# A decoder layer with routed experts on one core: row buffers twice, the first stage one step deeper, two expert loads late

## The chip, the cores and the metric

One core of a Trainium2 chip runs the whole layer in one launch. The metric is the device time of a run in microseconds (us). Three runs of the kernel before took 887.20, 883.02 and 879.79 us; the median is 883.02 us.

## The reference, cut to what matters

The input is x, 16 sequences of 256 tokens of width 256 (float32), and a context of the same shape. Three parts follow each other; each adds its input and normalizes it.

```python
# 1 attention of every sequence on itself
q, k, v = x@Wq.T + bq, x@Wk.T + bk, x@Wv.T + bv
qk = einsum('bsd,btd->bst', q, k)
theta = 0.5 + 0.2*sigmoid(qk) + 0.15*tanh(qk) + 0.1*relu(qk)
x1 = layernorm(x + (softmax(theta) @ v) @ Wo.T + bo)
# 2 cross attention to the context, 16 heads of 16, in chunks of 64 tokens
x2 = layernorm(x1 + out_proj(chunk_attention(x1, ctx)))
# 3 experts: 32 of them, 4 for each token, and a shared one
topk_idx, topk_w = route(x2)                  # sigmoid, best 2 of 4 groups, best 4 experts
h = silu(x2 @ gate_w[e].T) * (x2 @ up_w[e].T) # for the chosen experts e
out = layernorm(x2 + sum_e topk_w * h @ down_w[e].T + shared(x2))
```

## The kernel before, in words

All is float32. There are two stages, and a short last one.

**The first stage** goes over the 16 sequences in a software pipeline: `for t in range(nseq + 5)`, written out once for each engine (TensorE "PE" line 706, ScalarE "ACT" line 955, VectorE "DVE" line 1296, GpSimd "POOL" line 1413, the DMA queue of SyncE "SP" line 1490). In step t the engines work on sequence t (attention on itself: z, vo, scores1, prT, av1, x1T, and the context's k and v, and q), on sequence t-1 (cross attention: scores2, pTa, pTb, den, av2, spread, out2), on t-3 (router, shared expert, choice of experts, rank) and on t-4 (shared_out, and the scatter of the rows). Each engine works its list in the order in which it is written, and nothing overtakes; semaphores join the engines (`wait_ge`, and `after`, which waits only where the value is positive). The eight PSUM banks are shared out by hand, so many waits of PE stand for a bank that has to be read first.

In step t PE works in this order before: scores2(t-1), x2T(t-3), z, vo, scores1(t), shared_out(t-4), router, gate(t-3), pTa(t-1), k(t), prT(t), pTb(t-1), av1(t), up(t-3), av2, den(t-1), v(t), rank(t-3), x1T(t), spread(t-1), q(t), out2(t-1).

**Rows.** The normalized x2 of a sequence is copied four times, once for each chosen expert, into `row`, one buffer of [128, 4, 2, 258] (256 values, the weight, the number of the row in the result). POOL does this in `pool_row` (line 1377, copies at line 1382). DVE then writes weight and indices in `vec_key` (line 1178), and POOL scatters the rows to a DRAM tensor `routed`, sorted by expert, with eight indirect DMAs for each sequence (lines 1398 and 1405, "scattera" and "scatterb"). `pool_row` of the next sequence waits until all eight have landed. In POOL's list the order of a step is xc(t), rs2(t-3), scattera(t-4), xc2(t-1), scatterb(t-4), rs1(t), row(t-3). `act_norm2` (line 907) makes x2; what it needs from POOL is rs2.

**Queues.** SP issues the loads of the next sequence (xT, x, context), the store of the shared expert's part (`store_acc`), and `load_rest` (line 1463): in step 1 a write of 4128 KB of zeros to `routed` (line 1468), and in steps 1 to 16 the weights of two experts each (768 KB, line 1472). SP works in order too.

**The second stage** (`pe_tables` and the loops over 159 blocks of 128 rows) starts when the last scatter has landed: SP waits for it (lines 1503 and 1504) and then reads the first block (line 1511). PE also waits for all weights (`ld_we`). The last stage sums four results for each token and normalizes.

## Time and profile before

| | us |
|---|---|
| median of three runs (lowest, highest) | 883.02 (879.79, 887.20) |
| the profiled execution | 873.37 |
| its span | 871.2 |
| PE busy | 801.1 (92%) |
| DVE busy | 546.1 (63%) |
| ACT busy | 461.5 (53%) |
| POOL busy | 408.3 (47%) |

The span is the time from the first to the last thing that the profiler saw; the profiled execution took 2.2 us more than its span. "Busy" is the time in which an engine had an instruction in work. Matmuls are pipelined and overlap, so a busy PE says that it did not wait, not that it ran at its peak. The profile also gives the granted clock of TensorE as a share of full speed.

### The profile page before, as it was taken

The numbers are of one execution on the slowest core, as the hardware profiler recorded it, in microseconds if no ns is written. First come the engines' busy times: TensorE is split into PE (matmuls) and PEld (weight loads), VectorE is DVE, ScalarE is ACT, GpSimd is POOL, SyncE is SP. The second block draws the span as 40 slices with busy tenths as digits, with TensorE's granted clock in tenths as the row PEclk, the third lists the DMA queues.
The fourth block names the chain that finished last, engine by engine and source line by source line (L and its number), as shares of the span: only waits on it lengthen the run. The fifth ranks groups of instructions, "written<-read, shape, count | busy, mean of one in ns | idle before, by whom it ended". The sixth has DMA issues, their size and how long they took to land.

```text
span 871.2 us, 23658 instructions
## 1 busy us (share of the span) xinstructions
PE 801.1 (92%) x7881; PEld 658.8 (76%) x7881; DVE 546.1 (63%) x2115; ACT 461.5 (53%) x1150; POOL 408.3 (47%) x501
## 2 busy tenths in 40 slices
PE   7778999999999999999999555899999999999885
PEld 6567788888888888888887444688888888887332
DVE  2244577887788787887788852355555555554366
ACT  1455566655665666655665111466666666665133
POOL 0200235464455546464545662455656555556123
PEclk9999999999999999999999875999999999999999
DMA  6472223243324322342331124855555555552996
GB/s 222 125 174 79 80 69 103 100 136 93 121 76 142 106 103 82 133 124 94 104 127 58 67 86 134 301 163 166 165 162 159 169 165 158 161 170 91 327 401 242
DMA packets 69654, 125.06 MB, mean 144 GB/s; under 512 B 9665, under 2 KB 43329, under 8 KB 69282
## 3 DMA queue, kind: packets, MB, share of 16 engines
q1 hardware_dynamic: 51394, 81.60, 30.3%
q0 software_dynamic: 13776, 37.77, 12.1%
q10 hardware_dynamic: 4368, 4.20, 1.4%
q8 instruction: 67, 1.10, 0.5%
q14 instruction: 49, 0.40, 0.2%
HBM read 73.16 MB, written 50.36 MB: 142 GB/s over the span
## 4 chain that ended last, share of the span: by engine, by line
PE 78%; DMA 6%; POOL 5%; issue 4%; SPq 4%; ACT 2%; DVE 1%; ACTq 0%; POOLq 0%; DVEq 0%
PE banks L584 15%; PE banks L274 11%; PE banks L597 7%; PE banks L393 4%; SPq L623 4%; PE banks L381 3%; PE banks L354 3%; PE banks L314 3%; PE banks L335 3%; PE banks L371 3%; PE banks L326 3%; PE banks L487 3%; PE banks L518 3%; PE banks L541 3%; PE banks L529 3%
## 5 line engine op out<-in xcount | busy, mean ns | idle before, releaser
L1431 POOL DMA_INDIRECT y<-yb_tile,idcol_tile x159 | 153.0, 962 | 123.6 <-ACT yb_tile L948 121.3
L584 PE MATMUL banks<-w_expert_tile,xbT_tile 128*128 x636 | 166.4, 385 | 3.9 <-ACT xbT_tile L786 3.9
L584 PEld LDWEIGHTS banks<-w_expert_tile,xbT_tile 128*128 128x128 f32 x636 | 109.9, 193 | 13.5 <-issue 4.9
L1259 DVE COPY hbT_tile<-banks 128x128 f32<-128x128 f32 x159 | 46.4, 292 | 117.2 <-PE banks L274 117.2
L1398 POOL DMA_INDIRECT routed<-row_tile,idx_tile x64 | 63.3, 989 | 85.0 <-PE banks L410 66.5
L948 ACT ACTIVATE yb_tile<-banks,rowsb_tile 128x256 f32<-128x256 f32 x159 | 75.4, 474 | 48.8 <-PE banks L597 41.5
L597 PE MATMUL banks<-w_expert_tile,hbT_tile 128*128 x318 | 95.7, 383 | 0.0
L1366 POOL TENSOR_TENSOR rs_tile<-ve_tile,half_neg_tile 128x2 f32<-128x2 f32 x16 | 11.5, 717 | 140.6 <-DVE ve_tile L1046 140.6
L1405 POOL DMA_INDIRECT routed<-row_tile,idx_tile x64 | 65.7, 1027 | 17.7 <-issue 17.7
L942 ACT ACTIVATE gb_tile<-banks 128x128 f32<-128x128 f32 x159 | 44.2, 278 | 55.5 <-PE banks L584 55.5
L786 ACT ACTIVATE xbT_tile<-banks 128x256 f32<-128x256 f32 x159 | 59.9, 377 | 25.5 <-PE banks L274 25.2
L274 PE MATMUL banks<-const_tile,rowsb_tile 128*128 128x128 f32 x318 | 62.0, 278 | 6.9 <-DMA rowsb_tile<-routed 6.9
L274 PEld LDWEIGHTS banks<-const_tile,rowsb_tile 128*128 128x128 f32 x318 | 45.4, 144 | 23.9 <-DMA rowsb_tile<-routed 7.7
L597 PEld LDWEIGHTS banks<-w_expert_tile,hbT_tile 128*128 128x128 f32 x318 | 48.3, 192 | 12.6 <-issue 0.8
L649 PE MATMUL banks<-w_expert_tile,const_tile 128*128 128x512 f32 (+1 forms) x102 | 45.7, 596 | 8.1 <-DMA w_expert_tile<-y 8.1
L1242 DVE SCALAR_TENSOR_TENSOR hb_tile<-gb_tile,banks 128x128 f32<-128x128 f32 x159 | 44.6, 280 | 9.7 <-ACT gb_tile L942 9.6
L1246 DVE TENSOR_TENSOR hb_tile<-hb_tile,banks 128x128 f32<-128x128 f32 x159 | 45.6, 287 | 5.6
L649 PEld LDWEIGHTS banks<-w_expert_tile,const_tile 128*128 128x128 f32 x102 | 19.1, 196 | 35.2 <-DMA w_expert_tile<-y 17.8
L274 PE MATMUL banks<-const_tile,hb_tile 128*128 128x128 f32 x159 | 43.5, 274 | 0.0
L693 ACT ACTIVATE w_expert_tile<-w_expert_tile,fnmr_tile,frs_tile 128x256 f32<-128x256 f32 x32 | 17.6, 593 | 47.2 <-DVE fnmr_tile L673 47.2
L1382 POOL COPY row_tile<-x_tile 128x512 f32<-128x512 f32 x64 | 37.5, 625 | 6.9 <-DMA routed<-row_tile,idx_tile 6.9
L1360 POOL TENSOR_TENSOR xc_tile<-x_sb_tile,c_out_tile 128x256 f32<-128x256 f32 x32 | 23.0, 741 | 31.2 <-DVE c_out_tile L1311 27.4
(205 smaller groups left out, 1847.0 us busy)
## 6 DMA issues: line engine op xcount, KB each, us to landing
rowsb_tile<-routed SPq DMA_DIRECT2D x159, 129.0 KB, 2.2
w_expert_tile<-y SPq DMA_DIRECT2D x15, 1024.0 KB, 16.6
w_expert_tile<-w_expert SPq DMA_DIRECT2D x16, 768.0 KB, 6.3
cT_tile<-ctxT SPq DMA_DIRECT2D x16, 384.0 KB, 3.4
routed<-zrow_tile SPq DMA_DIRECT2D x1, 4128.0 KB, 22.7
xT_tile<-xT SPq DMA_DIRECT2D x16, 256.0 KB, 3.2
x_sb_tile<-x SPq DMA_DIRECT2D x16, 256.0 KB, 3.5
base<-acc_sb_tile SPq DMA_DIRECT2D x16, 256.0 KB, 3.8
```

Source lines behind the costliest of these rows:

```text
L274: return e.transpose(o, i, ident)
L584: m = e.matmul(bank[2 + u % 2][:, 0:2 * EI], xbT[u % 2][:, k * P:(k + 1) * P], w_flat[:, bass.ds(w + k * D, D)], start=k == 0, stop=k == D ...
L597: e.matmul(bank[6 + u % 2][:, 0:D], hbT[u % 2][:, :], w_flat[:, bass.ds(w + 2 * D, D)], start=True, stop=True).then_inc(SEM["p_down"], 1)
L649: m = e.matmul(sum_rows(g), ident, part(g, k), start=k == 0 and g >= 8, stop=k == TOPK - 2)
L786: e.activation(o, i, ACT.Copy).then_inc(SEM[done], 1)
L948: e.activation(yb[n % YS][:, :], bank[6 + u % 2][:, 0:D], ACT.Copy, scale=rowsb[n % ROWS][:, D:D + 1])\
L1242: e.scalar_tensor_tensor(hb1[u % 2][:, :], gb[u % 2][:, :], 1.0, bank[2 + u % 2][:, 0:EI], ALU.add, ALU.mult).then_inc(SEM["v_hb1"], 1)
L1246: e.tensor_tensor(hb[u % 2][:, :], hb1[u % 2][:, :], bank[2 + u % 2][:, EI:2 * EI], ALU.mult)\
L1259: e.tensor_copy(hbT[u % 2][:, :], bank[4 + u % 2][:, 0:EI]).then_inc(SEM["v_hbT"], 1)
L1398: e.indirect_dma_start(routed, bass.IndirectOffsetOnAxis(ap=idx[:, 0, k:k + 1], axis=0), row[:, k, 0, :], None).then_inc(SEM["st_rowa"], 16)
L1405: e.indirect_dma_start(routed, bass.IndirectOffsetOnAxis(ap=idx[:, 1, k:k + 1], axis=0), row[:, k, 1, :], None).then_inc(SEM["st_rowb"], 16)
L1431: e.indirect_dma_start(y, bass.IndirectOffsetOnAxis(ap=idcol[n % ROWS][:, :], axis=0), yb[n % YS][:, :], None).then_inc(SEM[f"st_y{n % YS} ...
```

## The change

`row` and `idx` become two buffers, taken in turn by even and odd sequences, and each has its own semaphores for the landed scatters. The four POOL copies become one ScalarE instruction, `act_row`, that reads x2 with a broadcast and writes all four copies (128 x 2048 elements). The pipeline is one step deeper, `range(nseq + 6)`: in step t the engines work on t (z, vo, scores1, k, v, prT, av1), t-1 (x1T, q), t-2 (all of cross attention), t-4 (router, gate, up, choice, rank) and t-5 (shared_out). kM, vM, mxa, rs1, nmr1, rs2, nmr2, r_sb, r_half, r_neg and den become two buffers each, rden becomes one. The PSUM banks are shared out anew, with new waits in nearly every function of PE. To make room, t12, prT, x1T and the second kM lie where the weights of the last four experts go, so these weights (the last two loads of 768 KB) are issued in steps 17 and 18 instead of 15 and 16, after waits for the last scores2, q, av1 and pr.

The orders of a step are written anew. PE: x2T(t-4), scores2(t-2), z, vo, scores1(t), router(t-4), k(t), gate(t-4), x1T(t-1), pTa, pTb(t-2), shared_out(t-5), v(t), den, av2, spread(t-2), up, rank(t-4), q(t-1), prT(t), out2(t-2), av1(t). ACT: x2T(t-4), z(t), norm1(t-1), vo(t), sha(t-2), tanh(t), sc(t-4), shb, pTa, pTb(t-2), x1T(t-1), pr(t), row(t-4), gates(t-4), num(t-2), norm2(t-3), q(t-1), prT, v, k(t). DVE: mxa(t-2), r(t), sha, mxb, shb(t-2), th(t), route(t-4), acc(t-5), rden(t-2), choice, hs1(t-4), o(t-2), key, hs2(t-4), x2(t-2), x1(t). POOL and SP stand in the diff. The second and the last stage are not changed.

The diff, cut to its core (bank numbers and waits of most PE functions are left out; two of them stand as examples):

```diff
@@ -143,51 +144,59 @@
+        SHARE = E // nseq * 3 * D
+        LATE = 3072 // SHARE
+
+        def late(at, n):
+
+            return w_flat[:, (nseq - LATE) * SHARE + at:(nseq - LATE) * SHARE + at + n]
...
+        t12 = late(0, 1024).rearrange("p (j t s) -> p j t s", j=2, t=T)
...
+        prT = late(1024, 512).rearrange("p (t u q) -> p t u q", t=T, u=T)
...
+        nmr1 = [sa(f"nmr1{u}", [P, T]) for u in range(2)]
...
+        x1T = late(2560, 512).rearrange("p (k s) -> p k s", k=DK)
...
-        kM = sa("kM", [P, DK, S // CH, 2, CH])
-        vM = sa("vM", [P, T, NP, VW])
-        mxa = sa("mxa", [P, 4, 4])
+        kM = [sa("kM0", [P, DK, S // CH, 2, CH]),
+              late(1536, 1024).rearrange("p (k n h c) -> p k n h c", k=DK, n=S // CH, h=2)]
+        vM = [sa(f"vM{u}", [P, T, NP, VW]) for u in range(2)]
+        mxa = [sa(f"mxa{u}", [P, 4, 4]) for u in range(2)]
...
-        row = sa("row", [P, TOPK, T, RW])
+        row = [sa(f"row{u}", [P, TOPK, T, RW]) for u in range(2)]
...
-        idx = sa("idx", [P, T, TOPK], I32)
+        idx = [sa(f"idx{u}", [P, T, TOPK], I32) for u in range(2)]
...
         def pe_z(e, i):
             e.wait_ge(SEM["ld_xT"], 16 * (i + 1))
-            after(e, SEM["a_pTb"], i - 1)
-            after(e, SEM["v_key"], i - 3)
             after(e, SEM["v_mx"], i)
+            after(e, SEM["v_ve2"], i - 2)
             for db in range(DK):
                 for k in range(DK):
-                    m = e.matmul(bank[1][:, db * S:(db + 1) * S], g_qk[:, k, db * P:(db + 1) * P], xT[:, k, :],
+                    m = e.matmul(bank[7][:, db * S:(db + 1) * S], g_qk[:, k, db * P:(db + 1) * P], xT[:, k, :],
                                  start=k == 0, stop=k == DK - 1)
             m.then_inc(SEM["p_z"], 1)
...
         def pe_vo(e, i):
             e.wait_ge(SEM["ld_xT"], 16 * (i + 1))
-            after(e, SEM["a_prT"], i)
-            after(e, SEM["a_q"], i)
-            after(e, SEM["a_x2T"], i - 2)
-            after(e, SEM["v_o"], i - 1)
+            after(e, SEM["a_k"], i)
+            after(e, SEM["a_q"], i - 1)
+            after(e, SEM["a_vo"], i)
+            after(e, SEM["a_x2T"], i - 3)
             for t in range(T):
                 for k in range(DK):
-                    m = e.matmul(bank[(0, 7)[t]][:, 0:D + 1], xT[:, k, t * P:(t + 1) * P],
+                    m = e.matmul(bank[(1, 6)[t]][:, 0:D + 1], xT[:, k, t * P:(t + 1) * P],
                                  g_vo[:, k, :], start=k == 0, stop=k == DK - 1)
             m.then_inc(SEM["p_vo"], 1)
...
@@ -398,9 +409,13 @@
             e.wait_ge(SEM["a_q"], i + 1)
             e.wait_ge(SEM["a_k"], i + 1)
             after(e, SEM["a_pTa"], i)
-            after(e, SEM["a_v"], min(i + 1, nseq))
-            after(e, SEM["a_x1T"], min(i + 1, nseq))
+            after(e, SEM["a_pTb"], i)
+            after(e, SEM["a_prT"], min(i + 2, nseq))
+            after(e, SEM["a_v"], min(i + 2, nseq))
             after(e, SEM["v_hs"], i - 2)
+            after(e, SEM["v_key"], i - 2)
+            after(e, SEM["v_o"], i)
+            after(e, SEM["v_rden"], i)
             for t in range(T):
                 for hf in range(DK):
                     for a in range(2):
...
         def pe_spread(e, i):
             e.wait_ge(SEM["v_rden"], i + 1)
-            after(e, SEM["v_rden"], min(i + 1, nseq))
+            after(e, SEM["a_pTb"], min(i + 1, nseq))
...
+        def act_row(e, i):
+            e.wait_ge(SEM["a_x2"], i + 1)
+            after(e, SEM[f"st_rowa{i % 2}"], 16 * TOPK * (i // 2))
+            after(e, SEM[f"st_rowb{i % 2}"], 16 * TOPK * (i // 2))
+            e.activation(row[i % 2][:, :, :, 0:D],
+                         x2[i % 2][:, :, :].rearrange("p (k t) d -> p k t d", k=1).to_broadcast([P, TOPK, T, D]), ACT.Copy)\
+                .then_inc(SEM["a_row"], 1)
 
         def act_norm2(e, i):
...
         def act_norm2(e, i):
             e.wait_ge(SEM["g_rs2"], i + 1)
-            after(e, SEM["g_row"], i - 1)
+            after(e, SEM["a_row"], i - 1)
...
@@ -1193,12 +1215,13 @@
             ch(e.tensor_tensor(mine[:, :, :, :], mine[:, :, :, :],
                                wraw[:, :, :].rearrange("p t (k x) -> p t k x", k=1).to_broadcast([P, T, TOPK, E]),
                                ALU.mult))
-            after(e, SEM["st_rowa"], 16 * TOPK * i)
-            after(e, SEM["st_rowb"], 16 * TOPK * i)
-            e.wait_ge(SEM["g_row"], i + 1)
-            e.tensor_scalar(idx[:, :, :], slot[:, :, 0:TOPK], -1.0, None, ALU.add).then_inc(SEM["v_idx1"], 1)
-            e.tensor_scalar(row[:, :, :, D + 1].bitcast(I32), row[:, :, :, D + 1].bitcast(I32), float(T), None, ALU.add)
-            e.tensor_reduce(row[:, :, :, D].rearrange("p k t -> p t k"), mine[:, :, :, :], AX.X, ALU.add)\
+            after(e, SEM[f"st_rowa{i % 2}"], 16 * TOPK * (i // 2))
+            after(e, SEM[f"st_rowb{i % 2}"], 16 * TOPK * (i // 2))
+            e.wait_ge(SEM["a_row"], i + 1)
+            e.tensor_scalar(idx[i % 2][:, :, :], slot[:, :, 0:TOPK], -1.0, None, ALU.add).then_inc(SEM["v_idx1"], 1)
+            e.tensor_scalar(row[i % 2][:, :, :, D + 1].bitcast(I32), row[i % 2][:, :, :, D + 1].bitcast(I32), float(2 * T), None,
+                            ALU.add)
+            e.tensor_reduce(row[i % 2][:, :, :, D].rearrange("p k t -> p t k"), mine[:, :, :, :], AX.X, ALU.add)\
...
-
-        def pool_row(e, i):
-            e.wait_ge(SEM["a_x2"], i + 1)
-            after(e, SEM["st_rowa"], 16 * TOPK * i)
-            after(e, SEM["st_rowb"], 16 * TOPK * i)
-            for k in range(TOPK):
-                m = e.tensor_copy(row[:, k, :, 0:D], x2[i % 2][:, :, :])
-            m.then_inc(SEM["g_row"], 1)
...
         def _(e):
-            e.iota(dest_id[:, :, :], [[N, TOPK], [1, T]], base=-T, channel_multiplier=TILES).then_inc(SEM["g_iota"], 1)
+            e.iota(dest_id[:, :, :], [[N, TOPK], [1, T]], base=-2 * T, channel_multiplier=TILES).then_inc(SEM["g_iota"], 1)
             e.wait_ge(SEM["v_setup"], 3)
             e.wait_ge(SEM["v_const"], 1)
-            for t in range(nseq + 5):
-                if live(t):
-                    pool_xc(e, t)
-                if live(t - 3):
-                    pool_rs2(e, t - 3)
+            for t in range(nseq + 6):
+                if live(t - 2):
+                    pool_rs1(e, t - 2)
+                if live(t - 1):
+                    pool_xc(e, t - 1)
+                if live(t - 6):
+                    pool_scatterb(e, t - 6)
                 if live(t - 4):
-                    pool_scattera(e, t - 4)
-                if live(t - 1):
-                    pool_xc2(e, t - 1)
-                if live(t - 4):
-                    pool_scatterb(e, t - 4)
-                if live(t):
-                    pool_rs1(e, t)
-                if live(t - 3):
-                    pool_row(e, t - 3)
+                    pool_rs2(e, t - 4)
+                if live(t - 6):
+                    pool_scattera(e, t - 6)
+                if live(t - 2):
+                    pool_xc2(e, t - 2)
             for n in range(BLOCKS):
...
@@ -1468,9 +1484,13 @@
                     e.dma_start(routed.rearrange("(e r) w -> r e w", e=E)[0:P, :, :],
                                 zrow[:, :].rearrange("p (e w) -> p e w", e=1).to_broadcast([P, E, RW]))\
                         .then_inc(SEM["st_zrow"], 16)
-                share = E // nseq * 3 * D
-                e.dma_start(w_flat[:, bass.ds(i * share, share)],
-                            d["w_expert"].rearrange("p e n -> p (e n)")[:, bass.ds(i * share, share)])\
+                if i == nseq - LATE:
+                    e.wait_ge(SEM["p_s2"], nseq)
+                    e.wait_ge(SEM["p_q"], nseq)
+                    e.wait_ge(SEM["p_av1"], nseq)
+                    e.wait_ge(SEM["a_pr"], nseq)
+                e.dma_start(w_flat[:, bass.ds(i * SHARE, SHARE)],
+                            d["w_expert"].rearrange("p e n -> p (e n)")[:, bass.ds(i * SHARE, SHARE)])\
...
@@ -1496,12 +1516,16 @@
                     load_c(e, t)
                 if live(t - 5):
                     store_acc(e, t - 5)
-                if live(t - 1):
+                if 0 < t <= nseq - LATE:
                     load_rest(e, t - 1)
+                if nseq < t <= nseq + LATE:
+                    load_rest(e, t - 1 - LATE)
             e.wait_ge(SEM["v_adr"], 1)
             e.wait_ge(SEM["st_zrow"], 16)
-            e.wait_ge(SEM["st_rowa"], 16 * TOPK * nseq)
-            e.wait_ge(SEM["st_rowb"], 16 * TOPK * nseq)
+            for u in range(2):
+                e.wait_ge(SEM[f"st_rowa{u}"], 16 * TOPK * nseq // 2)
+            for u in range(2):
+                e.wait_ge(SEM[f"st_rowb{u}"], 16 * TOPK * nseq // 2)
             for n in range(BLOCKS):
                 if n % UNROLL == 0:
...
```

## Rows read from the trace of the kernel before

**Rows 1.** The page: PE's busy share in tenths, in 40 equal slices of the span.
```profile
PE   7778999999999999999999555899999999999885
```

**Rows 2.** Stretches of the span: start:end, length, busy us (instructions) by engine, clock, DMA.
```profile
0.00:98.40 98.40, 78.00 (x829) 64.39 (x829) 35.16 (x99) 43.04 (x103) 12.30 (x25) 0.95 0.49 145
98.37:465.50 367.13, 366.91 (x5089) 320.26 (x5088) 294.29 (x1064) 226.61 (x521) 185.43 (x250) 1.00 0.32 103
353.20:381.50 28.30, 28.23 (x397) 24.75 (x392) 22.41 (x83) 17.44 (x40) 15.02 (x20) 1.00 0.35 107
465.50:532.00 66.50, 39.06 (x421) 30.84 (x420) 45.86 (x192) 10.92 (x19) 42.65 (x50) 0.81 0.23 80
```

**Rows 3.** Timeline of POOL, 478 to 520 us: start, length, instruction, idle before it.
```profile
481.87 2.50 POOL L1382 COPY row_tile<-x_tile 128x512 f32<-128x512 f32 x4 [3.08 <-DMA routed<-row_tile,idx_tile]
...
497.75 2.50 POOL L1382 COPY row_tile<-x_tile 128x512 f32<-128x512 f32 x4 [1.74 <-DMA routed<-row_tile,idx_tile]
...
519.51 0.98 POOL L1398 DMA_INDIRECT routed<-row_tile,idx_tile  x1 [0.98 <-DVE row_tile L1201]
```

**Rows 4.** Chain of waits at the change of stages: start, length, what.
```profile
528.50 2.48 DMA routed<-row_tile,idx_tile
...
532.00 2.06 DMA rowsb_tile<-routed
```

**Rows 5.** Timeline of PE in the first steps.
```profile
32.12 2.02 PE L381 MATMUL banks<-w_cross_tile,cT_tile 128*128 128x128 f32 x16
...
36.91 0.66 PE L274 MATMUL banks<-const_tile,x_tile 128*128 128x128 f32 x4 [2.77 <-ACT x_tile L903]
...
51.99 1.89 PE L274 MATMUL banks<-const_tile,sha_tile 128*128 128x128 f32 x8 [2.61 <-ACT sha_tile L875]
53.67 2.81 PE L371 MATMUL banks<-cT_tile,w_cross_tile 128*128 128x256 f32 x8
```

**Rows 6.** Timeline of PE in a full step: z and vo, each eight matmuls.
```profile
353.69 1.89 PE L314 MATMUL banks<-xT_tile,g_qk_tile 128*128 128x256 f32 x8
...
355.42 1.90 PE L326 MATMUL banks<-g_vo_tile,xT_tile 128*128 128x257 f32 x8
```

**Rows 7.** Timeline of SP's DMA issues in steps 0 and 1.
```profile
34.64 0.40 SPq L1468 DMA_DIRECT2D routed<-zrow_tile  x1
35.09 12.18 SPq L1472 DMA_DIRECT2D w_expert_tile<-w_expert  x1
49.41 0.33 SPq L1443 DMA_DIRECT2D xT_tile<-xT  x1
```

**Rows 8.** DMA issues of 35 to 50 us, with KB and us from issue to landing.
```profile
routed<-zrow_tile SPq DMA_DIRECT2D x1, 4128.0 KB, 22.7
w_expert_tile<-w_expert SPq DMA_DIRECT2D x1, 768.0 KB, 24.0
xT_tile<-xT SPq DMA_DIRECT2D x1, 256.0 KB, 10.4
```

**Rows 9.** Page, DMA issues of the whole run.
```profile
w_expert_tile<-w_expert SPq DMA_DIRECT2D x16, 768.0 KB, 6.3
xT_tile<-xT SPq DMA_DIRECT2D x16, 256.0 KB, 3.2
```

**Rows 10.** Instructions of ACT, by shape: busy, mean ns, idle before.
```profile
L875 ACT ACTIVATE sha_tile<-sha_tile 128x1024 f32<-128x1024 f32 x16 | 17.1, 1071 | 3.2 <-DVE sha_tile L1073 3.2
L786 ACT ACTIVATE num_tile<-banks 128x512 f32<-128x512 f32 x16 | 9.6, 603 | 18.3 <-PE banks L464 18.3
```

**Rows 11.** Timeline of DVE, 478 to 510 us, and rden of a full step (first row).
```profile
345.57 0.54 DVE L1096 RECIPROCAL rden_tile<-banks 128x64 f32<-128x64 f32 x1
...
485.17 0.68 DVE L1108 TENSOR_TENSOR xc_tile<-banks,xc_tile 128x512 f32<-128x512 f32 x1
...
490.18 0.20 DVE L1117 TENSOR_SCALAR sc_tile<-sc_tile 128x64 f32<-128x64 f32 x1 [0.32 <-ACT sc_tile L921]
...
500.71 0.41 DVE L1201 TENSOR_REDUCE row_tile<-mine_tile 128x8 f32<-128x256 f32 x1
```

428 lines of the change are left out of this document (215 added, 213 removed).

## The prediction

> **What bounds the kernel now.** I read the page first. PE is at 9 tenths from slice 4 on, with one hole at about 470 to 560 us, at the end of the first stage [rows 1]. The table of stretches says more [rows 2]. From 98.4 to 465.5 us PE stands still for only 0.2 of 367.1 us: these are 13 full steps, and one takes 28.3 us, in which PE is busy for 28.2, DVE for 22.4, ACT for 17.4 and POOL for 15.0. The fill, 0 to 98.4 us, holds 78.0 us of PE work. The drain, 465.5 to 532.0 us, holds 39.1 us of work in 66.5, at a clock of 0.81.
>
> The timeline of POOL shows what bounds the drain [rows 3]. The copies of one sequence start at 481.9, those of the next at 497.8: 15.9 us a sequence. Before them POOL has waited 3.1 and 1.7 us for the scatters to land, because there is one row buffer. rs2 stands behind the copies, and ACT's next x2, with the router behind it, waits for rs2. So copies, eight scatters and the landing run one after the other. Eight scatters take 10.2 us: the first of the last sequence starts at 519.5, the eighth at 528.5 [rows 3, 4], which is 1.28 us each. They land at 531.0, and SP reads the first block at 532.0 [rows 4]. From first scatter to that read is 12.5 us.
>
> **The sum in three parts.** "Before" is the profiled execution.
>
> Full steps. PE's work is the same, matmul for matmul, and POOL's 2.5 us of copies [rows 3] leave an engine that isn't the bound: nothing is gained there as long as PE covers all else. Added on ACT is one instruction of 2048 elements. 512 elements take 0.60 us and 1024 take 1.07 [rows 10], so it takes about 1.07 + 2 x 0.47 = 2.0 us, 19.4 of 28.3 in all. It stands between pr and gates. I laid ACT's new list against PE's new one with eight matmuls at 1.73 to 1.8 us [rows 6]: with x2T at 0, pTb ends at 13.6 and av2 at 19.3. ACT then does pTb, x1T, pr until 16.2, row until 18.2, gates until 18.8, and num can't start before 19.3. So row costs nothing; if it took 4.0 us it would still end before q's matmuls, the next that need the bank of num (22.5). Behind it, ACT ends v at 27.7 where scores2 of the next step wants it at 28.9. Not seen before are the new waits. Their bounds are 0 and, if a list is out of tune, the stalls in the second rival; I take 0, since every wait I placed ends 0.1 us or more before its use. The tightest is rden: den ends at 18.3, the reciprocal takes 0.54 [rows 11], the semaphores some 0.3, and spread wants it at 19.25.
>
> Fill. Before, step 0 runs through x1T and q of the same sequence, and PE waits for x1 (2.8 us) [rows 5]. That wait goes, since x1T and q belong to the next step now. Step 0 ends with v done earlier and av1 last, near 33.6, where v ended before at 34.1 [rows 5]. Step 1 has z, vo, scores1, k, q, av1 (six times 1.8), v (2.0) and two sets of four transposes (0.5 each) [rows 5, 6]: 13.8 us, and about 1.0 for the copy of prT on ACT ahead of av1. It ends at 48.4, scores2 at 49.6. What is late next is xT of sequence 2. SP issues the 4128 KB of zeros at 34.6 and the expert weights behind them, and is itself held in that issue for 12.2 us [rows 7]; they landed at 57.3 and 59.1, and xT, issued at 49.4, at 59.8 [rows 7, 8]. Now the zeros go out when v of sequence 0 is done, at about 30.4 instead of 34.1, so all this moves up by 3.5 us only: xT lands at 56.3, and PE waits 6.7 us. Step 2 has 13.8 us as step 1, pTa and pTb 1.8, den, av2, spread 3.0 and out2 1.8: 20.4. After the wait of 2.6 us before, eight transposes that take 1.04 elsewhere took 1.9 and the eight matmuls of k 2.8 instead of 1.9 [rows 5]: the clock was down, which costs about 2. Step 3 adds scores2 (1.2). So 56.3 + 20.4 + 2 + 21.6 = 100.3 us. Now the first step with x2T starts, as before at 98.4, but 12 instead of 13 steps are left to the end of step 15: 367.1 - 28.3 = 338.8. The drain begins at 439.1 instead of 465.5.
>
> The row of xT can be read in two ways: it queued behind the zeros, or it shared the bandwidth. The Trainium skill (DMA: Bandwidth & Descriptors, "Queues, rings and completion order") says that each DMA engine consumes the descriptors of a ring in ring order. By it the load has to wait for what is ahead, as in the sum. If it shared instead, a load issued at 43.8 (zeros at 30.9, weights at 31.3 and SP held for 12.2, then xT) would take its 10.4 us and land at 54.2, and the wait would be 2.1 us shorter.
>
> Drain. It is longer, since two cross attentions are left instead of one. Before, the step with scores2(15) took from 465.5 to the start of x2's last work at 485.2 [rows 11] and 2 us of statistics: 21.7. Two such steps, bound by DVE and PE in turn, overlap to 41.5 (21.9 and 19.6). Then come two steps with routing alone. DVE's chain of one, from route to the end of key, was 490.2 to 501.1, with acc ahead of it: 11 us [rows 11]. So key of the last sequence is ready at 63.5. POOL needs 10.2 us of scatters and 1 of rs2 for each, and has sequences 11 to 15 to do. Key ends 2.7 us (hs2 and x2) before the end of the two long steps, and 0.7 before that of the next, so I place 12 at 19.2 to 30.3, 13 at 38.8 to 49.9 (each with an rs2 between), 14 at 51.8 to 62.0; 15 starts at 63.5 and the read follows 12.5 later, at 76.0. Here the second buffer works: row(15) needs the scatter of 13, not of 14. The ends of this are 72 (DVE's key at its undisturbed length) and 82 (landings as slow as 4 us, slow clock in two steps). I add 1.5 us of slow clock, since the drain before ran at 0.81 [rows 2]: 77.5.
>
> The two late loads: they are issued behind store_acc of 12 and 13, about 31 and 46 us into the drain. One lands in 6.3 us [rows 9], so by 53 of 77.5. Their four waits are for PE and ACT work that is done by 22 us, and the stores behind them on SP aren't held. If that cover were gone, 6 us each. They may slow a landing by a few us; only row(15), with 5 us to spare, sees it.
>
> Sum: 439.1 + 77.5 = 516.6 us to the first read, against 532.0: 15.4 less. The second and last stage, 339.2 us, stay. The span would be 855.8, the profiled time 858.0. The profiled execution, 873.4, is 1.1% under the median of 883.0 and under all three runs; less 15.4 the median is 867.6. I forecast 868.
>
> **Rivals.**
>
> *The fill does not wait* (10%). If xT came before the zeros, 6.7 us and the slow clock's 2 go too: 859. Against it stands the landing 0.7 us after the weights.
>
> *PE loses its cover in the full steps* (13%, slower). Place: DVE's new list, mxa, r, sha, mxb, shb, th, route, acc, rden. Each waits for the one before, and rden stands behind route, about 3.6 us, and acc, which waits for shared_out at 15.4. If sc from ACT came 1 us later, rden would too, and spread, q, out2, av1, then x1 and the next step's sha would shift. From 15.4 / 12 = 1.3 us a step on the gain is gone. At 2.3 us, a whole th late (its four instructions), 27.6 are lost and 15.4 gained: 895. For it: PE had no gap before, so every microsecond shows. Against it: DVE has 5.9 us free in each step, ACT 8.9 with row.
>
> *The drain hands it back* (17%, about the same). If the scatters still went at 15.9 us a sequence, since the landing or x2 is tied as before, 13 to 15 would start at 35, 51 and 67 and the read come at 79.5 or, with late loads in the way of each landing (2 us each), 86: 8.5 more than forecast, 876. That would be the case in which the second buffer doesn't do what it is for.
>
> *The forecast's own case* (60%): 860 to 875, which leaves 0 to 0.6 us of stall in a full step.
>
> **How the numbers follow.** The forecast is 868. The range takes in the fill without wait (859) less the median's own play (the three runs lie within 7.4 us) and, above, the drain that hands it back (876) and mild stalls of up to 0.8 us a step (9.6: 878) with the same play: 857 to 883. It leaves out the strong stall. One per cent is 8.8 us, about what a measurement can tell here. Faster by that or more (under 874.2): forecast's case mostly (0.53 of 0.60), the fill (0.10), part of the rest (0.09): 0.72. Within: 0.17. Slower: 0.11.
>
> **What would show it.** The drain begins at 437 to 442 us, after 12 full steps of 28.3; if these are longer, the second rival is right, and the row of spread, pTa or q names what is late. PE waits about 6.7 us once, before z of step 2, for xT. `act_row` takes 2.0 us. In the drain, scatters of 14 and 15 follow each other almost without a gap, and ACT's row(15) waits for the scatter of 13. The first block is read at 513 to 521. I am wrong if PE shows gaps between 100 and 440, if the zeros end later than 54, or if the drain takes over 82.

## The result, and the profile after

The changed kernel is slower. Four runs took 924.09 us in the median (918.04 to 932.03) and four of the kernel before 881.40 (878.60 to 887.20). The ratio is 1.0453 of before, 95% interval 1.0367 to 1.0538; it is one of means and leaves out the slow run, 932.03. The forecast was 868 us.

The page has PE's busy share in tenths. Before, the nines ran on from slice 4 to the end of the first stage [rows 1]; now they break off again and again.

```profile
PE   7969889999987999989898885899999999999895
```

The table of stretches, cut where fill, full steps and drain end (start:end, length, busy us with instructions by engine, clock, DMA share, GB/s):

```profile
0.00:109.30 109.30, 88.07 (x888) 73.65 (x888) 41.79 (x117) 50.88 (x128) 13.66 (x27) 0.94 0.49 147
109.30:490.30 381.00, 348.81 (x4699) 306.49 (x4697) 272.52 (x985) 223.22 (x492) 142.40 (x184) 0.98 0.26 87
490.30:576.78 86.48, 64.04 (x749) 51.64 (x748) 60.40 (x258) 28.08 (x39) 43.91 (x50) 0.82 0.28 96
```

Twelve full steps take 381.0 us, 31.75 each, where 28.3 was forecast. PE is busy for 348.8 of them, so it stands still for 32.2 us; before, for 0.2 in 367 [rows 2]. PE is also busy for ten us more than 12 x 28.23; the mean granted clock of 0.98 over 381 us, against 1.00 before, accounts for about eight of them. The account, by the sums of the prediction, in us:

| | forecast | measured | more |
|---|---|---|---|
| x2T of the first sequence begins (end of the fill) | 100.3 | 108.9 | 8.6 |
| 12 full steps | 338.8 | 380.9 | 42.1 |
| drain, to the first block read | 77.5 | 87.0 | 9.5 |
| first block read | 516.6 | 576.8 | 60.2 |

The second and last stage took 345.8 us in this execution and 339.2 in that of before. The difference is not of the change: of the experiments, 1 to 4 show 346 to 348 and 5 to 17, which were run later, 338 to 340, and new and old kernels are among the later ones. So of the 51.4 us between the two profiled executions, 44.8 lie in the first stage. What else differs between the two sets of runs matters below, for den.

What PE waits for in the full steps (engine, what it was about to do, what it waited for: us in total, times, longest):

```profile
PE banks L458 <- issue: 12.3, 14, 1.2
PE banks L489 <- issue: 11.5, 6, 3.6
PE banks L520 <- ACT vo_tile L838: 4.2, 12, 0.5
PE banks L562 <- issue: 2.0, 1, 2.0
```

"issue" is a wait that no semaphore of the program explains. L458 is den, L489 spread, L562 rank. The timeline of PE in one step shows where they lie:

```profile
281.25 0.25 PE L458 MATMUL banks<-sha_tile,const_tile 128*32 128x64 f32 x2
...
282.94 0.22 PE L458 MATMUL banks<-shb_tile,const_tile 128*32 128x64 f32 x1 [1.15 <-issue]
...
284.53 0.94 PE L489 MATMUL banks<-rden_tile,const_tile 128*32 128x64 f32 x50
289.09 0.42 PE L489 MATMUL banks<-rden_tile,const_tile 128*32 128x64 f32 x14 [3.61 <-issue]
289.45 3.00 PE L542 MATMUL banks<-x2T_tile,w_shared_in_tile 128*128 128x256 f32 x8
```

PE stops in the middle of den and in the middle of spread, after 50 of 64 passes of matmuls that need nothing new. Behind the long gap up takes 3.00 us instead of 1.9: the granted clock was 1.00 until 290, 0.64 from 290 to 291 and 0.50 from 291 to 293 us, which is the lower level of 1.2 GHz for most of up, after 3.6 us of standing still. Den is not held by DVE. Its reciprocal (L1118) is what waits: 31.3 us in 12 steps, for den.

```profile
L1118 DVE RECIPROCAL rden_tile<-banks 128x64 f32<-128x64 f32 x12 | 6.7, 558 | 31.3 <-PE banks L458 31.3
```

What SP issues in the same step, and then, in the table of stretches of 1 us each (columns as above), how full the DMA engines are:

```profile
281.16 0.33 SPq L1476 DMA_DIRECT2D base<-acc_sb_tile  x1
281.52 0.48 SPq L1492 DMA_DIRECT2D w_expert_tile<-w_expert  x1
282.54 0.33 SPq L1459 DMA_DIRECT2D xT_tile<-xT  x1
282.92 0.49 SPq L1464 DMA_DIRECT2D x_sb_tile<-x  x1
283.50 0.55 SPq L1470 DMA_DIRECT2D cT_tile<-ctxT  x1
```

```profile
284.00:285.00 1.00, 1.00 (x88) 1.00 (x80) 0.90 (x5) 0.20 (x1) 0.00 (x0) 1.00 1.06 412
285.00:286.00 1.00, 0.48 (x33) 0.32 (x21) 0.90 (x6) 1.00 (x3) 0.00 (x0) 1.00 0.95 380
286.00:287.00 1.00, 0.00 (x0) 0.00 (x0) 0.56 (x1) 0.37 (x1) 0.49 (x1) 1.00 1.06 384
287.00:288.00 1.00, 0.00 (x0) 0.00 (x0) 0.00 (x0) 0.00 (x0) 0.91 (x2) 1.00 1.05 387
288.00:289.00 1.00, 0.00 (x0) 0.00 (x0) 0.00 (x0) 0.00 (x0) 0.00 (x0) 1.00 0.35 122
```

All loads of a step (256 + 768 + 256 + 256 + 384 KB = 1.9 MB) now go out in one bundle. In the kernel before, the context, the stored part and the weights went out at 346.7 to 347.5 and xT and x at 359.1 to 359.5. The cause is SP's order: `store_acc(t - 5)` kept its place in SP's list while acc moved in DVE's from t-4 to t-5. So SP stands in that store until the middle of the step, and the loads of the next step behind it. While the engines are full PE doesn't move, and it goes on when they become free.

### The profile page after: what moved, and what is told of

Read it like the earlier page. It is cut to its first block, busy times and chain, and to the rows that moved or that the text cites. A ratio compares the mean times of both kernels' runs of the same rounds, so it can differ in the third digit from the quotient of the medians.

```text
span 922.6 us, 23626 instructions
## 1 busy us (share of the span) xinstructions
PE 824.2 (89%) x7881; PEld 675.8 (73%) x7881; DVE 544.7 (59%) x2117; ACT 480.9 (52%) x1166; POOL 367.3 (40%) x437
## 3 DMA queue, kind: packets, MB, share of 16 engines
q1 hardware_dynamic: 51394, 81.60, 28.3%
## 4 chain that ended last, share of the span: by engine, by line
PE 70%; issue 9%; DMA 6%; SPq 5%; DVE 5%; ACT 3%; POOL 2%; another core or an unknown queue 0%; ACTq 0%; DVEq 0%; POOLq 0%
PE banks L596 13%; PE banks L283 10%; PE banks L609 8%; SPq L635 3%; PE banks L404 3%; PE banks L322 3%; PE banks L542 3%; PE banks L392 3%; PE banks L499 3%; PE banks L553 3%; PE banks L381 3%; PE banks L363 2%; PE banks L458 2%; PE banks L531 2%; DMA w_expert_tile<-y 2%
## 5 line engine op out<-in xcount | busy, mean ns | idle before, releaser
L1423 POOL DMA_INDIRECT routed<-row_tile,idx_tile x64 | 62.9, 983 | 38.1 <-issue 17.5
L1416 POOL DMA_INDIRECT routed<-row_tile,idx_tile x64 | 62.5, 977 | 22.6 <-issue 22.6
L881 ACT ACTIVATE qT_tile<-banks,b_cross_tile 128x256 f32<-128x256 f32 x32 | 13.4, 470 | 77.3 <-PE banks L404 77.3
L1409 POOL TENSOR_TENSOR xc_tile<-x_tile,c_out_tile 128x256 f32<-128x256 f32 x32 | 22.5, 722 | 75.7 <-issue 52.9
```

Source lines behind the costliest of these rows:

```text
L1416: e.indirect_dma_start(routed, bass.IndirectOffsetOnAxis(ap=idx[i % 2][:, 0, k:k + 1], axis=0), row[i % 2][:, k, 0, :], None).then_inc(SEM ...
L1423: e.indirect_dma_start(routed, bass.IndirectOffsetOnAxis(ap=idx[i % 2][:, 1, k:k + 1], axis=0), row[i % 2][:, k, 1, :], None).then_inc(SEM ...
```

## What could stop PE without a semaphore

Three things hold for these gaps. Nearly all fall among short matmuls or just behind them, where PE runs through 192 matmuls and 192 weight loads in some 3 us: den, av2 and spread stand directly behind each other now, where before v, rank and x1T stood between den and spread. In spread their place drifts and comes back every fifth step, three or four passes further on:

```profile
130.62 0.52 PE L489 MATMUL banks<-rden_tile,const_tile 128*32 128x64 f32 x18 [2.55 <-issue]
161.61 0.86 PE L489 MATMUL banks<-rden_tile,const_tile 128*32 128x64 f32 x42 [0.77 <-issue]
...
321.33 0.76 PE L489 MATMUL banks<-rden_tile,const_tile 128*32 128x64 f32 x39 [0.80 <-issue]
...
448.61 0.64 PE L489 MATMUL banks<-rden_tile,const_tile 128*32 128x64 f32 x11 [3.58 <-issue]
481.20 0.75 PE L489 MATMUL banks<-rden_tile,const_tile 128*32 128x64 f32 x36 [0.22 <-issue]
```

With the one at 289.09, of 14 passes, these are pairs five steps apart: 18 and 14 and 11 passes left, 42 and 39 and 36. A semaphore would stop PE at the same instruction in each step; this place counts instructions. And the kernel before has the same kind of gap, in its fill, where no up stands ahead of av2 and den, with the DMA engines idle from 61 to 63 us:

```profile
63.00 0.25 PE L447 MATMUL banks<-sha_tile,const_tile 128*32 128x64 f32 x2 [1.88 <-issue]
```

The page lists a DMA queue for instructions, 67 packets with 1.10 MB, 16.4 KB each. So the theory (A) is: PE's instructions come by DMA in blocks; a run of short instructions uses up a block before the next is there, and full DMA engines make that later. The rivals: B, only the run counts; C, only the DMA counts; D, since the gap in den stands at nearly one place, after 20 to 23 of 64 passes (after 28 in the first step that has it), that one has another cause, POOL's scatters, of which the eighth runs beside it. In the first of the 12 full steps no scatter runs yet, and den has no gap.

A is more than a guess, since the trace holds every packet of that queue. The long gap above lasts from 285.48 to 289.09 us. The queue's last packet before it started at 272.3, the next at 286.83, and PE went on 1.27 us after that one had landed. Here is what the queue of instructions moved in 286.8:287.9 (packets, MB, share of the engines):

```profile
q8 instruction: 1, 0.02, 5.6%
```

It is PE's queue: 38 of its packets fall in the 12 full steps, one for each 247 of PE's matmuls and weight loads, and all six gaps in spread, the one in rank and the one in q end 1.3 to 1.5 us after such a packet has landed. The gaps in den do not follow it: that of 281.79 to 282.94 has no packet of this queue within 8 us before it or 3 us behind it. So A is shown for spread, rank and q, and not for den.

The Trainium skill (Runtime: NRT & Kernel Launch, "Instruction fetch mechanics") describes blocks of 16 KiB that a sequencer fetches through its own DMA queue, and calls the cost "mostly hidden". The size of the packets agrees; the 11.5 us of gaps in spread do not.

## Experiments

Ratios are to runs of the kernel before on the same chip, with 95% intervals. Medians of before lay at 880 us beside experiments 1 to 4 and at 870 beside the later ones, so only ratios are compared. The changed kernel and 1 to 4 are the first set of runs, 5 to 17 the later one. 16 rests on two runs; the others have 4 to 12.

| | ratio | interval |
|---|---|---|
| the changed kernel | 1.0453 | 1.0367 to 1.0538 |
| 1 store one turn later | 1.0341 | 1.0273 to 1.0409 |
| 2 and the other loads after spread | 1.0210 | 1.0173 to 1.0248 |
| 3 changed kernel, up before spread | 1.0359 | 1.0306 to 1.0412 |
| 4 = 2 + 3 | 1.0174 | 1.0121 to 1.0227 |
| 5 changed kernel, scatters first | 1.0112 | 1.0056 to 1.0168 |
| 6 = 4 + scatters first | 0.9919 | 0.9892 to 0.9946 |
| 7 4, av2 before den | 1.0019 | 0.9994 to 1.0044 |
| 8 4, eighth scatter held | 0.9985 | 0.9962 to 1.0008 |
| 9 4, shared_out before den | 1.0024 | 1.0005 to 1.0044 |
| 10 = 6 + zeros in four parts | 0.9831 | 0.9804 to 0.9859 |
| 11 10, row waits for the last scatters | 1.0095 | 1.0067 to 1.0124 |
| 12 before, up behind den | 1.0134 | 1.0083 to 1.0185 |
| 13 before, loads beside av2 and den | 1.0073 | 1.0042 to 1.0104 |
| 14 = 12 + 13 | 1.0156 | 1.0100 to 1.0212 |
| 15 before, eighth scatter beside den | 1.0030 | 1.0006 to 1.0054 |
| 16 before, two scatters beside den | 1.0155 | 1.0111 to 1.0198 |
| 17 before, den first beside scatters | 1.0036 | 1.0007 to 1.0064 |

### 1 to 4: the loads and the long run

1, SP in the changed kernel:

```diff
-                if live(t - 5):
-                    store_acc(e, t - 5)
+                if live(t - 6):
+                    store_acc(e, t - 6)
```

> The changed kernel, with one thing moved: SP issues the store of the shared part one turn later (store_acc(t-6) for store_acc(t-5)), so that SP is not held in it and the loads of xT and x go out early in a step again; the context's load and the weights still follow v, just ahead of den, av2 and spread. In the trace of the changed kernel the PE gaps in den and spread (12.3 + 11.5 us between 109 and 490 us) fall together with a bundle of 1.9 MB of DMA. Theory A (a run of some 200 short PE instructions outruns PE's own instruction loads, and full DMA engines make that load late): the bundle shrinks to about two thirds, the gaps in spread shrink by about half, 924 -> about 912 us. Rival B (the run of short instructions alone is enough, DMA traffic has no part): unchanged, 920 to 927. Rival C (DMA alone, whatever PE executes): as A or more, 905 to 912.

2 adds, in `load_c`:

```diff
                 after(e, SEM["p_v"], i)
+                after(e, SEM["p_spread"], i - 2)
```

> As e1, and SP also waits for spread before it issues the context's load and, behind it, the stored part and the weights: no large transfer is on its way while den, av2 and spread run. Theory A: what is left are short gaps of about 1 us a step like those that the kernel before shows with idle DMA at 63 and 91 us; the long ones of 2.6 to 3.6 us are gone: about 900 us. Rival B: as the changed kernel, 920 to 927. Rival C: no gap is left in den and spread at all, full steps of 28.3 us, about 885 us.

3, PE in the changed kernel:

```diff
-                if live(t - 2):
-                    pe_spread(e, t - 2)
                 if live(t - 4):
                     pe_up(e, t - 4)
+                if live(t - 2):
+                    pe_spread(e, t - 2)
```

> The changed kernel with SP as it is, and PE's order changed in one place: the eight long matmuls of up stand ahead of spread, so that den and av2, then up, then spread follow each other instead of den, av2, spread, up. Theory A: the 1.9 us of up give the instruction load time in the middle of the run: gaps in spread go, those in den stay with their 0.5 to 1.2 us: 924 -> about 908. Rival B (length of the run alone): the same, or better, about 900. Rival C (DMA alone): the stalls only change place: 918 to 925.

> e2 and e4 together: no large transfer during den, av2 and spread, and up in the middle. Theory A: full steps near 28.5 us, what stays is the longer fill and drain: about 885 us. Rival B: as e4. Rival C: as e2.

Measured: 1 takes 1.1 points off and 2 another 1.3; the intervals of the changed kernel and of 2 lie far apart, those of the changed kernel and of 1 or 3 overlap, so for these two the traces speak and not the time. Between 100 and 490 us PE's gaps in spread are 5.6 us in 1 (longest 2.2) and 3.9 in 2 (longest 1.6), against 14.1 with 3.6. 3 takes 0.9 points off, with 5.6 us left in spread (longest 2.7). So B falls: DMA traffic makes the gaps long. C falls too, by 2: a gap of 1.62 us stands in spread while the DMA engines do nothing (second row).

```profile
275.28 0.42 PE L489 MATMUL banks<-rden_tile,const_tile 128*32 128x64 f32 x14 [1.62 <-issue]
```

```profile
274.00:275.00 1.00, 0.00 (x0) 0.00 (x0) 0.84 (x3) 0.55 (x2) 0.31 (x1) 1.00 0.00 0
```

The packets of instructions say how the traffic does it. The gap that ends at 275.28 and the one of 3.61 us in the changed kernel stand at the same instruction, with 14 passes left. In 2 the packet starts 0.9 us before PE stops, in the changed kernel 1.35 us after; it lasts 1.2 and 1.0 us, and PE goes on 1.3 us behind it in both. So the block isn't moved more slowly beside the bundle, it starts 2.2 us later, and the gap is 2.0 us longer. When PE's sequencer asked for it is not in the trace. In all kernels here, old and new, the gaps of 0.4 us and more between 35 and 500 us in the runs of short matmuls and just behind them end 0.9 to 1.6 us after such a packet has landed. The exceptions are den in the first set of runs and one wait of q in 11.

In 4 spread has no gap at all after 100 us. The sizes were off: 885 us was expected of 4 and 897 came. What is left is den, 13.8 us between 100 and 490, and nearly so large in all four kernels (12.9, 12.3, 10.9, 13.8). A full step of 4 takes 30.05 us, with 1.07 of gap in den and 0.33 of a wait of router for ACT's vo.

### 5 to 9: the gap in den

```profile
270.86 0.22 PE L458 MATMUL banks<-shb_tile,const_tile 128*32 128x64 f32 x1 [1.08 <-issue]
```

```profile
269.07 0.96 POOL L1416 DMA_INDIRECT routed<-row_tile,idx_tile  x1 [0.30 <-issue]
```

In 4 den starts at 269.24, 0.17 us after the eighth scatter (second row), stops 0.5 us later and goes on 0.8 us after that scatter's instruction has ended. 5 and 6 change POOL's order, in the changed kernel and in 4:

```diff
-                if live(t - 1):
-                    pool_xc(e, t - 1)
                 if live(t - 6):
                     pool_scatterb(e, t - 6)
...
                 if live(t - 6):
                     pool_scattera(e, t - 6)
+                if live(t - 1):
+                    pool_xc(e, t - 1)
```

> The changed kernel with one move on POOL: xc(t-1) stands behind the eight scatters instead of ahead of them, so that they end about 2.5 us earlier and the last one no longer runs beside the start of den. In the changed kernel and in the two kernels with later loads, den stops for about 1.1 us in every step after its first 11 or 12 matmuls, with the DMA engines nearly idle, and goes on when POOL's last scatter has moved its data; in the drain it does so for 2.9 us beside two scatters. Theory D (short matmuls stall beside POOL's indirect DMAs): the 12 gaps in den go, the gaps in spread stay: 924 -> about 910. Rival (den's place behind v is what makes it stall, or the load of PE's instructions alone): den's gaps stay, 918 to 926.

> The kernel of the fifth experiment (loads after spread, up ahead of spread) with the same move on POOL. There a full step took 30.05 us, 1.07 of them the gap in den and 0.33 a wait before router. Theory D: a step takes about 28.7 us, 897 -> about 881, and a little more in the drain. Rival (place in PE's list): 895 to 898.

The gaps in den are gone in both. 5 gains 3.4 points, twice what was expected, although 12.3 us of gaps in spread stay: those are shorter (1.2 to 2.2 instead of up to 3.6). Their packets of instructions start no later than 0.04 us after PE has stopped; that spread now comes before the bundle has filled the DMA engines is the likely reason. The move also ends router's wait for vo, 0.3 us in all in both kernels instead of 4.2 and 4.0. 6 is faster than the kernel before. Two kernels were to place the cause. In 7 den and av2 change places; in 8 only the eighth scatter is moved (`after(e, SEM["p_av2"], min(i + 4, nseq))` before its issue), xc and the loads stay.

> The kernel with loads after spread and up ahead of spread (30.05 us a step, 1.07 of them a gap in den beside the last scatter), with den and av2 exchanged: v, av2, den, up, spread. The scatters are where they were. Theory D1 (any short matmuls stall beside the last of eight scatters): now av2 stops, after some 11 matmuls, for about 1.1 us; time unchanged. Theory D2 (only den stalls, whose matmuls accumulate in 32-row groups): av2 runs through, and den, 0.9 us later, stops for 0.2 us or not at all: about 12 us less. Theory D3 (only what stands directly behind v stalls, scatters or not): as D1; D1 and D3 are told apart by the kernels with earlier scatters, where den stands behind v and did not stop.

> The kernel with loads after spread and up ahead of spread (30.05 us a step), with one wait more on POOL: the eighth scatter of a sequence waits for av2, so that nothing of POOL runs beside den; xc, the load of x and the other seven scatters stay as they are. If the scatter beside den is what stops it: the gaps in den go, a step of about 28.9 us, 0.015 of before less (ratio about 1.003). If the move of xc and with it of x's load was what helped: the gaps stay, 1.017.

In 8 all gaps in den go, and in 7 av2, in den's place, runs through. By the expectations that would be D and D2. 9 exchanges v and shared_out on PE:

> The kernel with loads after spread and up ahead of spread (30.05 us a step, gap of 1.07 in den beside the eighth scatter), with v and shared_out exchanged on PE, so that den stands behind eight long matmuls as in the kernel before, at the same time and beside the same scatter. If the short matmuls of v ahead of den belong to the stall: no gap, ratio about 1.002. If they don't (the new order's banks or tiles do): the gap of 1.07 stays, about 1.017.

No gap in den there either, though den begins 0.7 us after the scatter instead of 0.17, since v now lost 0.29 us in each step.

But these five kernels can't decide it, because no later run has the gap at all, not even where the scatters lie beside den as they did in 4. The drain shows it. In 4 den starts at 473.49 us, with scatters 0.38 us before and 0.97 us behind its start; in 8 at 458.72, with scatters 0.39 before and 0.95 behind. PE's order around it is the same. These are the rows of den alone (start:end, length, busy us with instructions of PE and of its weight loads, clock, DMA share, GB/s), first 4, then 8:

```profile
473.40:479.10 5.70, 2.71 (x64) 1.59 (x64) 0.91 0.40 142
458.60:459.90 1.30, 1.10 (x64) 0.94 (x64) 1.00 0.00 0
```

Den stops five times for 0.4 us or more in the one and never in the other. It is the same in both long steps of the drain in all kernels that have den ahead of av2: with scatters starting during den or less than 1 us before it, it has gaps in the changed kernel and in 1 to 4, and none in 5, 6, 8, 9, 10 and 11. In the first set each gap of 0.4 us and more in den begins 0 to 1.4 us after a scatter has started, and steps without scatters have none, so a scatter does belong to it; but so does something that the first set had and the later one hadn't. It isn't the chip alone, since 9 ran on the chip of 1 to 4. The second stage, whose code is the same in all of them, shows the same division, with 346 to 348 us in the first set and 338 to 340 in the later one. What it is stays open, and so does how much of the gain of 5 to 9 comes from the moves: 4 was not run again beside them.

### 12 to 17: the same in the kernel before

12 moves one call on PE, `pe_up(e, t - 3)`, from ahead of av2 to behind den.

> The kernel before with one call moved on PE: up stands behind den instead of ahead of av2, so that av1 is followed by av2 and den at once, as in the fill, where PE stopped 1.9 us in den in both steps. SP and POOL as before. Theory A (a long run of short instructions outruns PE's instruction loads, if a boundary of 256 instructions falls so that the next load begins only with the run): gaps in some of the 13 steps, 1 to 2 us each, 880 -> 884 to 895. Rival (gaps need full DMA engines or POOL's scatters): no gap, 878 to 882.

It does what A says: five gaps of up to 2.1 us in den between 100 and 460 us and one of 1.1 in up, about 12 us more time, with SP and POOL untouched.

13 lets `load_xT` wait for av1 as well and puts `load_rest` ahead of `load_c`.

> The kernel before, with SP alone changed: the loads of xT and x wait for av1 as well, and the weights' load goes right behind them, so that 1.3 MB are on their way while PE does up, av2 and den; PE's order as before. Theory A: the loads of PE's instructions have time in up and av1, so gaps in den come only where a boundary falls badly, 0 to 1 us a step: 0 to 8 us longer. If full DMA engines alone stop PE: gaps of 1 us and more in each step, 13 us and more longer. If DMA traffic does nothing without a long run: no change.

> The kernel before with both edits that were run alone: up behind den (1.0134 of before, gaps of 1.2 to 2.1 us in 6 of 13 full steps) and the loads of xT, x and weights at the end of av1 (1.0073, gaps of 0.2 to 1.5 us in 5 of them). If full DMA engines delay the loads of PE's instructions: the gaps at the same places grow to 2.5 to 3.6 us, as in the changed kernel, and the sum is more than that of the two, about 1.03. If the two don't act on each other: 1.02, gaps as they were.

13: five gaps in spread, 3.0 us in all, and 0.7 points. 14: no more than 12, 9.7 us of gaps for 8.5, longest 2.3. So the interaction expected at 2.5 to 3.6 us did not show; SP issues at 289.3 us and the gap there begins at 290.8, and the packet of instructions starts at 290.6, when the engines are 0.29 busy. So the block is on its way before the bundle fills them. That the bundle lengthens the gaps rests on 1 and 2 and on the packets there.

15, 16 and 17 put scatters beside den in the old order: the eighth alone; the seventh and eighth; both, with den ahead of av2.

> The kernel before with one wait more: the eighth scatter of a sequence waits for the end of up, and so runs beside av2 and den, where POOL was idle; the other seven stay. PE's order and SP's are those of before. Theory D: PE stops in av2 or den for about 1 us in each of 13 full steps, as nowhere before: 880 -> about 893. Rival (place in PE's list): no gap, 878 to 882.

> The kernel before, with the seventh and the eighth scatter of a sequence held until up is done (one alone, the eighth, made no gap). So two scatters in a row run beside av2, den and v. If it takes two in a row: gaps of 0.5 to 1.1 us in den in each full step; if den behind av2 is safe in any case: none. rs1 comes 1.3 us later in either case, and x1T with it, so the time is 0 to 13 us longer even without gaps; the trace decides, by the rows of av2 and den.

> The kernel before, with den ahead of av2 on PE (it then stands behind up, eight long matmuls), and with the seventh and eighth scatters held until av1 is done, so that the eighth runs beside den's start as in the changed kernel. If den first among the short matmuls, beside a scatter, is all it takes: a gap of about 1.1 us in den in each of 13 full steps, 1.016 of before. If not: no such gap, and something else of the new order belongs to it.

None makes the gap in den, but all three are of the later set, which shows it nowhere. In 17 den starts at 284.41, 0.12 us after the eighth scatter at 284.29, as in the changed kernel, and runs through. 16 is slower otherwise: its full steps take 28.9 to 30.2 us, with x1T waiting for x1 behind the late rs1 (2.7 us in 11 times), and none of it is a gap in den. So D in its general form, that short matmuls stop beside any scatter, is wrong; whether the old order would have the gap in the first set's condition was not run.

### 10 and 11: the best version, and what the second buffer gives

10 writes the zeros in four parts, in `load_rest` (POOL's first scatter waits for the last part):

```diff
-                if i == 0:
+                if i < 4:
...
-                    e.dma_start(routed.rearrange("(e r) w -> r e w", e=E)[0:P, :, :],
-                                zrow[:, :].rearrange("p (e w) -> p e w", e=1).to_broadcast([P, E, RW]))\
+                    e.dma_start(routed.rearrange("(e r) w -> r e w", e=E)[0:P, i * E // 4:(i + 1) * E // 4, :],
+                                zrow[:, :].rearrange("p (e w) -> p e w", e=1).to_broadcast([P, E // 4, RW]))\
```

> The kernel with all three moves (loads after spread, up ahead of spread, xc behind the scatters), and the 4128 KB of zeros written in four parts, one behind the loads of each of the first four sequences, so that xT of sequence 2 doesn't stand behind all of them; POOL's first scatter waits for the last part. In the trace of the three moves PE waits 6.5 us for that xT, and the clock is low for 3 us behind it. Expected: the wait goes and no other comes: 862 -> about 854, 0.982 of before. If the weights' load behind each part holds xT as long: no change.

855.63 us, 0.9831 of before: the fastest kernel here. PE's wait for xT is gone. Its full steps and its drain, in the table of stretches:

```profile
94.46:436.19 341.73, 339.76 (x4697) 298.00 (x4696) 270.59 (x983) 223.48 (x493) 146.51 (x184) 1.00 0.31 101
436.19:513.88 77.69, 58.28 (x753) 46.32 (x751) 59.88 (x262) 28.63 (x40) 44.10 (x50) 0.89 0.31 107
```

A full step takes 28.48 us, and the drain 77.7. The last scatter of sequence 14 and the first of 15 on POOL, and row(15) on ACT, which waited for the scatters of 13:

```profile
499.83 1.08 POOL L1416 DMA_INDIRECT routed<-row_tile,idx_tile  x1 [0.30 <-issue]
501.41 0.96 POOL L1425 DMA_INDIRECT routed<-row_tile,idx_tile  x1 [0.51 <-DVE row_tile L1224]
```

```profile
491.44 1.91 ACT L923 ACTIVATE row_tile<-x_tile 128x2048 f32<-128x2048 f32 x1 [0.97 <-DMA routed<-row_tile,idx_tile]
```

11 takes the second buffer's effect away, in `act_row`:

```diff
             after(e, SEM[f"st_rowb{i % 2}"], 16 * TOPK * (i // 2))
+            after(e, SEM[f"st_rowa{(i + 1) % 2}"], 16 * TOPK * ((i + 1) // 2))
+            after(e, SEM[f"st_rowb{(i + 1) % 2}"], 16 * TOPK * ((i + 1) // 2))
```

> The best version so far (three moves and the zeros in four parts, 855.6 us, 0.983 of before), with act_row(i) made to wait also until the scatters of i-1 have landed: two buffers that are used as if there were one. In the drain of the best version the scatters of 14 start 10.7 us before those of 15, and row(14) is written while those of 13 run. With the wait row(14) starts at 491.4 in place of 480.3, its scatters 3.6 us later, and row(15) only when they have landed: its scatters start 7.3 us later. In the full steps row waits 0.5 us and nothing of PE waits for it. Expected: 7 us more, 0.991. If the second buffer is worth nothing: no change.

It costs not 7 but 23.8 us (first block at 537.6 instead of 513.9), 2.6 points. POOL, first scatter of 14 and of 15:

```profile
507.20 0.96 POOL L1427 DMA_INDIRECT routed<-row_tile,idx_tile  x1 [8.27 <-DVE row_tile L1226]
...
525.20 0.95 POOL L1427 DMA_INDIRECT routed<-row_tile,idx_tile  x1 [7.99 <-DVE row_tile L1226]
```

A sequence takes 18 us there: x2 of the next one waits for row, and x2T, router, key, scatters and landing follow one after the other. The expectation had only moved row.

## Why the prediction was wrong, step by step

**Full steps: the failed step.** The prediction took 28.3 us for each, since "every wait I placed ends 0.1 us or more before its use". All but one did: the only semaphore that shows in the 12 steps is router's for vo, 4.2 us, 0.35 a step, which the sum had at 0. What the sum did not have is the supply of PE's instructions. It laid the lists of ACT and PE against each other by durations and counted den, av2 and spread as 3.0 us wherever they stand. The experiments showed two prices of their standing together: gaps from the length of the run (12 makes them in the old kernel, 4 takes them away in the new), and their growth under SP's bundle (1, 2). In the 12 steps these are 11.5 us in spread, 2.0 in rank and 1.8 in q, and behind the long ones ten us more of busy time, about eight of them by the low clock. The 4.2 of router's wait and 12.3 of den, whose cause is open, make up the 42 us more. The failed step alone is enough to make the forecast wrong: 5, with no gap in den, is 1.1% slower than before, where 1.7% faster was forecast. In 6, a step takes 28.5 us, as in 10.

**SP's order** was a miss of the same step. Of the moved acc, the prediction followed the buffers and banks, not the store of it; of SP it looked only at the two late loads. The store holds xT, x, context and weights of every step. On its own that made no wait, xT was always in time; it made the bundle.

**The second rival** was right in sign, short in size (2.3 us a step for 895 us; it was 3.5), and wrong in its place: DVE was not late, it waited for den. **"I am wrong if PE shows gaps between 100 and 440"** was the sentence that decided it.

**act_row** took 1.91 us where 2.0 was said, and nothing waited for it. In 5 it stands just ahead of den as before, and den runs.

**Fill.** PE waited 7.9 us for xT of sequence 2, and z started at 57.0:

```profile
56.99 3.78 PE L322 MATMUL banks<-xT_tile,g_qk_tile 128*128 128x256 f32 x8 [7.89 <-DMA xT_tile<-xT]
```

6.7 and 56.3 were forecast, by the reading that xT stands behind the zeros; if it had shared the bandwidth it would have been 54.2. The Trainium skill (DMA: Bandwidth & Descriptors, "Queues, rings and completion order") has the ring served in order, and the trace agrees. The expert weights, issued at 31.1, and xT behind them, issued at 42.4, took from issue to landing (last number, us):

```profile
w_expert_tile<-w_expert SPq DMA_DIRECT2D x1, 768.0 KB, 25.0
xT_tile<-xT SPq DMA_DIRECT2D x1, 256.0 KB, 14.6
```

So the weights landed at 56.1 and xT at 57.0, where its 10.4 of before would have given 52.8. In 10, with the zeros in four parts, PE's wait for this xT is gone. The two steps behind took 8 us more than forecast: gaps in spread of 1.2 and 2.6, the low clock behind them and behind xT, and waits of 0.2 to 0.4 for vo and shb.

**Drain.** 77.5 us forecast, 87.0 measured. Here too den stopped (it took 4.1 us instead of 1.1 in the first of the two long steps, and 2.8 in the second), and the mean granted clock was 0.82, against 0.89 in 10. In 6 and 10, where den does not stop, the drain takes 77.6 and 77.7. Row(15) waits for the scatters of 13, as said. The scatters of 14 and 15 do not follow each other at once in the changed kernel: 3.6 us lie between them (560.7 to 564.3), in which POOL waits for DVE's key; in 10 it is 0.5, where the sum had 1.5. So the mechanism was right and the size came out only without den's gaps, and 11 shows that the second buffer is worth 23.8 us in 10's drain; the third rival had put the loss of it at 8.5.

**What stays open** is what, besides the scatter, belongs to the gap in den, 12.3 of the 42 us. It is in all five kernels of the first set and in none of the later one, whatever the place of den. Late instructions are not it: in 4, den stops from 269.78 to 270.86 with no packet of PE's instructions since 264.8, and in others a packet has just landed, with no difference in the gap. To settle it, 4 and 8 would have to run side by side in both conditions.

## What to carry to other kernels

A list that is written by hand has a supply of instructions behind it: put long instructions between runs of short ones, look for gaps "<- issue" whose place drifts from step to step, and then for the packets of the instruction queue beside them. When a step moves by one iteration, follow its store through the queue that issues it: what stands behind it moves too, and loads that were spread come as a bundle. A saving in the drain is real only if the full steps stay as they were; here 3.5 us in each of 12 steps ate nearly twice what the second buffer gave. The moves of 6 and 10 ended below the kernel before; how much of that the absence of den's gap in the later runs gave is not separated. Hence the last rule: when a gap goes after an edit, run the kernel that had it again beside the new one.

## What was not expected of the hardware

A run of 192 matmuls and 192 weight loads in some 3 us stopped TensorE for 1.6 to 2.0 us with idle DMA engines and for up to 3.6 us at 380 to 412 GB/s, and TensorE went on 0.9 to 1.6 us after a packet of its instructions had landed. After the 3.6 us of standing still the granted clock stayed at 1.00 for the first microsecond of work and was 0.64 and then 0.50 in the next three. Beside an indirect DMA of GpSimd, a run of 128x32 matmuls stopped for about 1.1 us in every such full step of one set of runs; in the drains of a later set, with the same instructions at the same distance from the DMA, it did not stop at all.
